# ScalarE's copy of each r block of attention, moved from behind the relative copy to between two halves of the exponentials of the next eighth

## The reference, cut to what matters

```python
def _L0_conv_ref(x, wq, wk, wv, wo, rq, rk, rv, Gq, Gk, Gv1, Gv2):   # x is 4 x 256 x 128 x 128
    q = _conv1x1(wq, x).reshape(n, NH, HD, H, W)                      # NH 16 heads of HD 16 channels
    k = _conv1x1(wk, x).reshape(n, NH, HD, H, W)
    v = _conv1x1(wv, x).reshape(n, NH, HD, H, W)
    qk = jnp.einsum('nhcij,nhciw->nhijw', q, k) / D
    qrq = jnp.einsum('nhcij,chjw->nhijw', q, rq) / D
    krk = jnp.einsum('nhcij,chjw->nhijw', k, rk) / D
    weight = jax.nn.softmax(qk + Gq * qrq + Gk * krk, axis=3)
    out = jnp.einsum('nhijw,nhciw->nhcij', weight, Gv1 * v) + jnp.einsum('nhijw,chjw->nhcij', weight, Gv2 * rv)
    return _conv1x1(wo, out.reshape(n, C, H, W))
...
x = x + _L0_conv_ref(_ln_c(x), ...)
t = _to_tokens(x)
t = t + _L0_ffn_ref(_ln_t(t), ...)     # 64 experts, each takes its 8 best tokens of every image
```

## Time and profile before

| | |
|---|---|
| median of 3 runs | 7508.54 us (7497.94 to 7526.4) |
| the profiled execution | 7515.16 us, span 7513.4 us |
| granted TensorE clock, mean of the span | 0.913 |
| busy: TensorE matmul / weight loads | 6392.3 us (85%) / 4983.2 us (66%) |
| busy: VectorE / ScalarE / GpSimd | 5358.7 (71%) / 4722.5 (63%) / 2483.9 us (33%) |
| attention | about 1528 to 5888 us of the span |
| exponentials, L697 | 8192 of 394 ns mean, 2515.0 us |
| relative copies, L690 | 1024 of 1008 ns, 1032.5 us; 323.7 us idle before them |
| r copies, L704 | 512 of 597 ns, 305.9 us; 387.5 us idle before them |

### The profile page before, as it was taken

One profiled execution on the slowest core, in us unless ns is written; L12 is line 12 of the kernel. 1 busy time (PEld: TensorE's weight loads), 2 busy tenths in 40 slices (PEclk: granted clock), 3 DMA queues, 4 the chain that ended last, 5 costly groups with the idle time before them and its releaser, 6 DMA issues. The chain is left out here.

```text
span 7513.4 us, 279833 instructions
## 1 busy us (share of the span) xinstructions
PE 6392.3 (85%) x106442; PEld 4983.2 (66%) x106442; DVE 5358.7 (71%) x20905; ACT 4722.5 (63%) x11171; POOL 2483.9 (33%) x1267
## 2 busy tenths in 40 slices
PE   4999999979989999889998999989999766576558
PEld 3555555568878888788887888878888433232258
DVE  5444444448878888788887888878888788898820
ACT  0444444358988888888888888888888334333300
POOL 0000000025545545445544454444544322232110
PEclk7999999969999999999999999999999988898755
DMA  7555555557677677767777677767766667686422
GB/s 217 202 205 206 206 205 205 180 89 125 122 130 128 117 130 130 123 117 128 127 121 129 119 124 130 126 121 121 134 120 116 207 228 231 193 264 196 143 96 95
DMA packets 1197409, 1146.43 MB, mean 153 GB/s; under 512 B 625632, under 2 KB 956000, under 8 KB 1194144
## 3 DMA queue, kind: packets, MB, share of 16 engines
q1 hardware_dynamic: 1006816, 842.59, 54.1%
q10 hardware_dynamic: 188352, 285.27, 10.3%
q0 software_dynamic: 1024, 2.09, 0.1%
HBM read 708.04 MB, written 421.56 MB: 150 GB/s over the span
## 5 line engine op out<-in xcount | busy, mean ns | idle before, releaser
L790 POOL TENSOR_TENSOR att_scores<-att_scores,att_inverse 128x1024 f32<-128x1024 f32 x1024 | 1993.8, 1949 | 2139.3 <-DVE att_inverse L738 2138.8
L697 ACT ACTIVATE att_scores<-att_scores,att_negmax 128x128 f32<-128x128 f32 x8192 | 2515.0, 394 | 26.1 <-issue 20.8
L753 DVE CUSTOM_DVE_ANT_0 att_scores<-att_ps,att_scores 128x128 f32<-128x128 f32 x8192 | 1817.8, 289 | 831.9 <-PE att_ps L614 803.0
L603 PE MATMUL att_ps<-att_qk,att_rs 32*128 32x64 f32 x32768 | 2174.1, 280 | 80.5 <-DMA att_qk<-qk 38.7
L614 PE MATMUL att_ps<-att_own 32*128 32x128 f32 x16384 | 1811.2, 322 | 338.0 <-ACT att_scores L690 166.4
L603 PEld LDWEIGHTS att_ps<-att_qk,att_rs 32*128 32x128 f32 x32768 | 2022.5, 195 | 88.0 <-issue 81.3
L614 PEld LDWEIGHTS att_ps<-att_own 32*128 32x128 f32 x16384 | 1595.2, 197 | 654.5 <-issue 334.0
L656 PE MATMUL att_ps<-att_scores,att_rv 128*16 128x64 f32 x32768 | 1391.0, 331 | 18.7 <-issue 16.6
L736 DVE TENSOR_REDUCE att_total<-att_scores 128x8 f32<-128x1024 f32 x1024 | 1241.4, 1212 | 0.0
L690 ACT ACTIVATE att_scores<-att_ps 128x1024 f32<-128x1024 f32 x1024 | 1032.5, 1008 | 323.7 <-PE att_ps L603 322.4
L656 PEld LDWEIGHTS att_ps<-att_scores,att_rv 128*16 128x16 f32 x32768 | 1129.8, 119 | 41.3 <-issue 31.1
(11 more groups left out here) (147 smaller groups left out, 5072.9 us busy)
## 6 DMA issues: line engine op xcount, KB each, us to landing
qk<-proj_qk_out ACTq DMA_DIRECT2D x64, 2048.0 KB, 8.6
att_qk<-qk SPq DMA_DIRECT2D x512, 256.0 KB, 5.9
att_own<-qk SPq DMA_DIRECT2D x1024, 128.0 KB, 4.3
proj_x<-in_x_dram SPq DMA_DIRECT2D x128, 512.0 KB, 4.3
v_t<-proj_v_out ACTq DMA_DIRECT2D x64, 1024.0 KB, 11.4
att_vt<-v_t SPq DMA_DIRECT2D x256, 256.0 KB, 5.2
att_v<-att_att_v SPq DMA_DIRECT2D x1024, 64.0 KB, 3.7
att_r<-att_att_r SPq DMA_DIRECT2D x1024, 64.0 KB, 2.6
```

Of the source, the lines that this page charges most:

```text
L603: return pe.matmul(ps[:, 4 + gg, jj * IU:(jj + 1) * IU], rs[32 * g:32 * g + 32, j, :], qk[v % 2][32 * g:32 * g + 32, :, j, :], start=True, ...
L697: last = act.activation(scores[v % BUFS][:, i, :], scores[v % BUFS][:, i, :], ACT.Exp, bias=negmax[v % BUFS][:, i:i + 1], scale=-1.0)
L753: last = dve.tensor_tensor_reduce(out=scores[v][:, i, :], in0=ps[:, 2 * (p % 2) + r // HR, (r % HR) * W:(r % HR + 1) * W], in1=scores[v][: ...
L790: pool.tensor_tensor(piece(scores[v], p), piece(scores[v], p), piece(inverse[v], p).unsqueeze(3).broadcast_to([P, 2, HR, W]), ALU.mult).th ...
```

## The change

ScalarE's program of a unit is written in another order. The copy of a block of r sums no longer stands behind the relative copy of the odd eighth in which TensorE ends the block, but in the even eighth that follows, between its first four exponentials and its second four. In terms of `p`: blocks 2 and 3 of the unit two back were read at `p` 1 and 3 and are now read at 2 and 4, blocks 0 and 1 of the unit one back were read at 5 and 7 and are now read at 6 and, in the next unit, at 0. The waits of the copy itself, and all other engines' programs, stay as they are.

```diff
--- before.py
+++ after.py
@@ -706,21 +706,19 @@
             def unit(u, v, parts):
                 back2, back1, now, ahead1, ahead2 = parts
                 for p in range(PIECES):
-                    if p == 0:
-                        if back1:
-                            exp_half(u - 1, v - 1, HALVES - 2)
-                            exp_half(u - 1, v - 1, HALVES - 1)
-                    elif now:
-                        exp_half(u, v, 2 * p - 2)
-                        exp_half(u, v, 2 * p - 1)
+                    for half in range(2):
+                        if p == 0 and back1:
+                            exp_half(u - 1, v - 1, HALVES - 2 + half)
+                        if p and now:
+                            exp_half(u, v, 2 * p - 2 + half)
+                        if half == 0 and p % 2 == 0 and p < 6 and back2:
+                            read_r(u - 2, 1 + p // 2)
+                        if half == 0 and p == 6 and back1:
+                            read_r(u - 1, 0)
                     if p < 6 and ahead1:
                         read_relative(u + 1, v + 1, p + 2)
                     if p >= 6 and ahead2:
                         read_relative(u + 2, v + 2, p - 6)
-                    if p % 2 and p < 4 and back2:
-                        read_r(u - 2, 2 + p // 2)
-                    if p % 2 and p >= 4 and back1:
-                        read_r(u - 1, p // 2 - 2)
 
             for t in range(ROUNDS):
                 read_relative(0, 0, t)
```

## The result

The changed kernel takes 7450.7 us (median of 6 runs, 7431.39 to 7467.59) against 7505.8 (6 runs, 7497.09 to 7526.4): ratio 0.9929, 95% interval 0.991 to 0.9947. That is 0.7% faster, some 55 us, where 151 were forecast (7358), and 5.7 us above the upper end of the range. The interval leaves out 1, so the gain is real, though small. The profiled execution took 7456.45 us, its span is 7454.4.

The account below looks back on a forecast made before the run. A ring between ScalarE's r copy and TensorE's odd eighth was taken as the bound. Saving 0.36 us in 419 pairs, 151 us, takes 7515.2 to 7364; less 6.6 for the median, 7358 us, range 7290 to 7445.

Parts of the forecast that it names:

- The ring: Attention: r copy, exponentials, relative copy and TensorE's odd eighth wait on each other in a loop of 7.71 us a pair.
- median pair: Two successive eighths in attention: TensorE alone needs 7.32 us for them, so r copies should come 7.3 us apart.
- 0.28 gap: TensorE's idle time before each eighth's weight loads, put down to issue; counted as its own and expected to stay.
- first rival: TensorE's 0.28 us gaps before eighths go too, VectorE's 7.06 us a pair bounds: 289 us gained, 7220 us; chance 0.08.
- third: VectorE or ScalarE eats part in attention: pairs run at 7.5 us, half the gain goes, 7435 us; chance 0.12.
- fourth: The wait only moves, to the exponentials or the relative copy, some 0.7 us a pair: 7508 us; chance 0.06.
- last: Slower: TensorE's r sums wait for the late r copy and bank 7, 41 us more: 7550 us; chance 0.05.
- second: Head changes gain as well, if SP was waiting for engines: 184 to 220 us, about 7305 us; chance 0.06.
- 0.36 x 419 = 151 us: Total gain in attention: TensorE's avoidable wait for the relative copy, 0.36 us a pair, over 419 gaining pairs.
- the heads: At 15 head changes SP's queue sets the time: 93 of 512 pairs gain nothing, own-load waits grow about 2.7 us each.
- stalls put down to issue: TensorE's attention idle time without a named cause, 296.8 us with the 0.28 gaps; used to choose between two gain estimates.
- the smaller of two estimates: Attention gain by TensorE's waits, 151 us, taken over 180 us by 11 quiet pairs.

Follow-up runs that it names:

- e4: Changed kernel without the eight small loads of the next head's gain at each head change (results not the reference's): 7377.4 us, ratio 0.9833.
- e2: Kernel before, with the q and k loads for the relative scores in contiguous 8 KB pieces instead of 256 B ones: 7406.8 us, ratio 0.987.
- e1: Changed kernel, with the q and k loads for the relative scores in contiguous 8 KB pieces instead of 256 B ones: 7343.3 us, ratio 0.9785.
- e10: Kernel before, with q and k loads spread into the next unit and a head's gain brought by one DMA: 7407.8 us, ratio 0.9875.
- e7: Changed kernel, with q and k loads spread into the next unit and a head's gain brought by one DMA: 7348.5 us, ratio 0.9805.
- e12: Changed kernel with q, k and v loads cut, plus added DRAM-to-DRAM copies in 256 B pieces: 7406.3 us, ratio 0.9886.
- e16: Changed kernel with q, k and v loads cut, plus 16 added DRAM-to-DRAM copies of 256 KB a unit in large pieces: 7665.5 us, ratio 1.0224.
- e13: Changed kernel with only the own q and k loads cut to 1/4 of their bytes: 7190.6 us, ratio 0.9591.

## Why the prediction was wrong

The sign, the bound and the mechanism were right; the sum was not, and the sum gave the range.

**What bounded.** The ring of the earlier trace rows was the bound and went; the median pair is 7.31 us where 7.32 was forecast. TensorE is the next bound, although its weight loads are busy only 3541.12 of 4302 us (82%). Its 0.28 gap is its own (first rival refuted). VectorE doesn't eat half of the gain (third): it still stands 748.4 us for TensorE before its adds. The wait doesn't move to the exponentials (fourth): they stand 9.4 us for `negmax`. And no r sums wait for the copy beyond 5.3 us (last). The heads didn't gain either (second).

**The term that was mis-sized.** "0.36 x 419 = 151 us", in three parts. First, what TensorE no longer waits for: forecast 0.36 x 512 = 184, measured 176.8 - 29.1 = 148. The weight loads' row, 269.8 / 397 less 0.28 = 0.40 an event, overstates it a little; the matmuls' row has 166.4 / 442 = 0.38, and 29.1 us stayed, 10.4 of them before L603 in both orders. Second, the heads: forecast -33, measured 150.0 - 125.1 = -25 (1.7 us a head, where the prediction had 2.7). The step holds, and e4 shows its cause. Third, and most of the miss, what was not in the sum: the prediction took the "stalls put down to issue" as the same before and after, and used them only to choose the smaller of two estimates. They grew by 57 us. 148 - 25 - 57 = 66 against 58 of attention; small rows and 3 us of busy time make the rest.

**Where the 57 come from.** Three things are shown. The issue waits are waits for TensorE's instructions, which come by DMA (796 blocks of 16 KB in queue q8, 13.04 MB, in the kernel before): they end 1.2 to 2.0 us behind the landing of a block. They come from the loads of q, k and v: with all three light 18.6 and 18.1 us are left in the two orders, and with them their difference goes, and in the new order most of them go already with either of the two big loads. And they follow how often the DMA engines are full: in the new order 19 us at 0 to 5 full stretches of 925, 40 and 30 at 78 and 126, 110 at 179, 133 at 191, 149 to 174 at 214 to 270.

Why the change makes them more is measured, and its reading is argued. Take the blocks from 1700 to 5400 us that start behind 3 us in which the engines were busy for 90% or more, and call one late when it is the last to land before an issue wait. The change hardly alters how many blocks start so, 267 and 264, but 61 of them are late before and 104 after. It is so in the two other pairs of runs: 44 of 265 in e2 and 85 of 244 in e1, 71 of 253 in e10 and 112 of 248 in e7. (The longer full stretches of the table are 225 before and 263 after, but 200 and 179, and 239 and 239, in the two other pairs.) So the engines are about as full as they were, and the same full stretch stops TensorE more often. The reading is that TensorE, which stood 0.4 us in every pair, left a block that much more time to come. No run varies that pause alone.

The Trainium skill ("Runtime: NRT & Kernel Launch", Instruction fetch mechanics) has TensorE's instructions streamed in blocks of 16 KB by a DMA queue of its own, and the cost mostly hidden. The 16 KB packets of q8 agree; the cost is not hidden here, 99.6 us before and 156.4 after the change. The Trainium skill ("DMA: Bandwidth & Descriptors", Queues, rings and completion order) also has each DMA engine take turns between the queues it has work for, packet by packet. No run here shows in which order an engine serves them.

**What stays open.** Where a late block loses its time: its own transfer is only a little longer (median 1.50 us against 1.19 of the other blocks in the changed kernel), and when it was asked for is in no row. Whether copies between DRAM tensors would hold it up as loads onto the chip do: e12 and e16 did not fill the engines for long. A run with fewer TensorE instructions in the same time, or one with a pause put into TensorE's program, was not tried.

## What to carry to other kernels

When an engine that was held becomes the bound, every small stall that it used to swallow in the wait counts: add the rows put down to issue to the list of what is late next, and look how often the DMA engines are full beside them. The mean share doesn't tell: at 0.58 one run had 78 full stretches of 4 us and another 3. A saving of waits is best taken from the row of the engine that will be the bound, summed over the stage, not from a quiet pair. And a stretch in which SP issues without a gap keeps nearly its length whatever the engines do (56.7 and 55.9 us); taking eight tiny DMAs out of it was worth about as much as the change itself (73 us by the medians, 54 to 72 by the ratios, against 55 and 53 to 71).

## What the hardware showed that was not expected

- The idle time put down to issue before TensorE's attention matmuls follows the full stretches of the table in both orders, and the mean DMA share less well: at 0.58 it is 40 us in e13 and 19 in e12.
- A DMA of 0.1 KB holds SP's queue as long as one of 256 KB: the median issue of a gain load takes 0.36 us and that of a v load 0.35, with single ones up to 1.9 and 2.4. It is their number that costs: eight gain loads held the queue for 5.97 us, four own loads of 128 KB for 1.81 or 4.39.
- With light loads TensorE's same 98304 matmuls were busy for 3831 us instead of 3954, at a granted clock of 0.97 instead of 0.94.
- ScalarE's extra change between exponential and copy costs nothing to be seen: the copy at 3017.13 starts 1.21 us behind four exponentials of 1.31 and hands on after 0.48.
